# Where the node features are loaded and turned, and what the slot gathers signal on, in a two-layer graph kernel

## The reference, cut to what matters

```python
Hb = einsum('ni,bio->bno', h, V)
coef = w_comp[etype]
m = sum(coef[:, b] * Hb[b][src] for b in range(4)) * norm      # norm is edge_weight
agg = segment_sum(m, dst)
hn = relu(agg + h @ loop_w + bias)
y = hn @ ffn_w.T + ffn_b + h
x = layernorm(x + layernorm_with_gain(y))                      # first layer
x = layernorm(x + conv2(relu(conv1(x))))                       # attention over the edges
```

## Time and profile before

| what | us |
|---|---|
| median of 3 runs | 2035.97 (2034.86 to 2036.61) |
| the profiled execution | 2030.42 |
| its span in the profile | 2028.5 |
| TensorE matmul busy in the span | 1952.3 (96%) |
| VectorE busy | 1431.0 (71%) |
| ScalarE busy | 1297.1 (64%) |
| GpSimd busy | 671.6 (33%) |
| `message`, first row of the weight matrix built until the last feature sum | about 52 to 1057 |
| the two `conv` stages | 1067 to 1547 and 1548 to 2028 |

### The profile page before, as it was taken

One profiled execution on the slowest core, in us unless ns is written; L12 is line 12 of the kernel. 1 busy time (PEld: TensorE's weight loads), 2 busy tenths in 40 slices (PEclk: granted clock), 3 DMA queues, 4 the chain that ended last, 5 costly groups with the idle time before them and its releaser, 6 DMA issues. The chain is left out here.

```text
span 2028.5 us, 53132 instructions
## 1 busy us (share of the span) xinstructions
PE 1952.3 (96%) x19165; PEld 1633.2 (81%) x19165; DVE 1431.0 (71%) x4127; ACT 1297.1 (64%) x2289; POOL 671.6 (33%) x802
## 2 busy tenths in 40 slices
PE   1799999999999999999989999999999999999998
PEld 1789999999999999999975777777776777777777
DVE  3888878878887887888635666666663766677665
ACT  1566766767676676767645666666664666666665
POOL 3676577566657656665210000000000000000000
PEclk8899999999999999999999999999999999999999
DMA  3012111111211111121013222222211233222220
GB/s 80 9 38 76 42 40 52 65 39 39 77 40 40 53 64 39 39 78 37 34 67 128 96 69 90 95 95 84 73 63 71 94 104 103 84 87 101 102 102 8
DMA packets 43018, 137.00 MB, mean 68 GB/s; under 512 B 9190, under 2 KB 24359, under 8 KB 36484
## 3 DMA queue, kind: packets, MB, share of 16 engines
q1 hardware_dynamic: 38484, 128.24, 17.7%
q0 software_dynamic: 4400, 6.80, 1.4%
HBM read 91.83 MB, written 43.20 MB: 67 GB/s over the span
## 5 line engine op out<-in xcount | busy, mean ns | idle before, releaser
L854 PE MATMUL ps<-matrixT,x_rows 125*128 125x256 f32 (+1 forms) x2500 | 563.5, 377 | 0.1
L1703 DVE CUSTOM_DVE_ANT_0 scores_l<-ps,bias_rows_l 125x500 f32<-125x500 f32 (+1 forms) x700 | 396.6, 619 | 212.5 <-issue 212.5
L854 PEld LDWEIGHTS ps<-matrixT,x_rows 125*128 125x128 f32 x2500 | 461.3, 190 | 48.4 <-issue 0.2
L1608 ACT COPY weightsT_l<-ps 125x500 f32<-125x500 f32 x400 | 230.4, 577 | 293.4 <-PE ps L1514 292.8
L945 ACT COPY matrixT<-ps 125x500 f32<-125x500 f32 (+2 forms) x800 | 381.9, 652 | 44.3 <-PE ps L842 44.3
L1514 PEld LDWEIGHTS ps<-eye,scores_l 125*125 125x125 f32 x2500 | 287.8, 188 | 114.5 <-issue 106.7
L842 PE MATMUL ps<-high_weights,low_onehot 64*125 64x125 f32 x6300 | 368.2, 275 | 11.1 <-DVE high_weights L722 11.1
L842 PEld LDWEIGHTS ps<-high_weights,low_onehot 64*125 64x125 f32 x6300 | 357.9, 189 | 24.7 <-issue 15.8
L1514 PE MATMUL ps<-eye,scores_l 125*125 125x125 f32 x2500 | 324.9, 280 | 1.3 <-ACT weightsT_l L1608 1.3
L1600 ACT ACTIVATE scores_l<-scores_l,neg_max_l 125x1500 f32<-125x1500 f32 x200 | 318.0, 1594 | 7.5 <-DVE neg_max_l L1738 7.5
L1499 PE MATMUL ps<-kT_l,q_tile_l 64*125 64x500 f32 (+1 forms) x1400 | 317.0, 564 | 1.5 <-DVE chunk_max_l L1703 1.2
(11 more groups left out here) (152 smaller groups left out, 1725.7 us busy)
## 6 DMA issues: line engine op xcount, KB each, us to landing
bias_rows_l<-bias SPq DMA_DIRECT2D x50, 1562.5 KB, 6.7
bias<-bias SPq DMA_DIRECT2D x75, 500.0 KB
x_rows<-in_x SPq DMA_DIRECT2D x1, 1562.5 KB
bias<-bias SPq DMA_DIRECT2D x25, 62.5 KB
x<-x_rows SPq DMA_DIRECT2D x25, 62.5 KB
x_rows_l<-x SPq DMA_DIRECT2D x25, 62.5 KB
out<-rows_l SPq DMA_DIRECT2D x25, 62.5 KB
dst_int<-in_dst SPq DMA_DIRECT2D x1, 402.8 KB
```

The source lines that it names most:

```text
L854: last = nc.tensor.matmul(psG[:, BASES * SPLIT * side:BASES * (SPLIT * side + SIDE[side])], x[:, h, :], MT[side][:, 0:SIDE[side], BASES * ...
L1608: nc.scalar.copy(PT[i][:, 0:cw[c]], psT[i % 3][0:R, 0:cw[c]]).then_inc(z["pa_ok"], 1)
L1703: V.tensor_tensor_reduce(S[par][:, hd, lo:hi], psS[2 * ((par + j) % 2) + hd][0:R, 0:cw[j]], bias[par][0:R, lo:hi], 1.0, FLOOR, ALU.add, AL ...
```

## The change

The load of `x` leaves `prepare`. In `message` the sync engine issues it behind the 25 weight loads. (`prepare`'s other branch, for irregular graphs, which these inputs don't take, issues it ahead of its weights.) TensorE and ScalarE no longer turn `x` at the head of `message`; they do it in step 3, behind the first half of tile 0's pair products and their evacuation, and before the digits of tile 1 are turned. The seventh and eighth PSUM tile take the place of the first two. The four gathers of a tile's slots signal on two semaphores: destination and source on one, type and weight on the other. `slot_kinds` waits for the first, makes the digits, then waits for the second and makes `kinds`; `kinds_ok` is raised by the last row of `kinds`.

```diff
-def turn_inputs(nc, pe, m, turned_ps, turned_ok):
+def turn_inputs(nc, pe, m, turned_ps, turned_ok, at=0):
-    x, eye, ps = m["x"], m["eye"], m["ps"]
+    x, eye, ps = m["x"], m["eye"], m["ps"][at:at + 2]
...
-def turned_out(nc, act, m, turned_ps, turned_ok):
+def turned_out(nc, act, m, turned_ps, turned_ok, at=0):
-    xT, ps = m["xT"], m["ps"]
+    xT, ps = m["xT"], m["ps"][at:at + 2]
...   prepare, sync engine
-            sp.dma_start(m["x"][:, :, :], a["x"].rearrange("(t p) f -> p t f", p=R)).then_inc(m["x_in"], 16)
...   message
-        ell_in = [sem("ell_in0"), sem("ell_in1")]
+        near_in, kind_in = [sem("slot_ends_in0"), sem("slot_ends_in1")], [sem("slot_kinds_in0"), sem("slot_kinds_in1")]
...   message, gpsimd, find_slots
-                for to, name in ((e_dst, "dst"), (e_src, "src"), (e_type, "edge_type_8"), (e_weight, "edge_weight")):
+                for to, name, landed in ((e_dst, "dst", near_in), (e_src, "src", near_in), (e_type, "edge_type_8", kind_in),
+                                         (e_weight, "edge_weight", kind_in)):
...
-                                                 in_offset=bass.IndirectOffsetOnAxis(ap=slot_at[par][:, :], axis=0)).then_inc(ell_in[par], 16)
+                                                 in_offset=bass.IndirectOffsetOnAxis(ap=slot_at[par][:, :], axis=0)).then_inc(landed[par], 16)
...   message, sync engine
             load_weights(nc, sp, a, m)
+            sp.dma_start(m["x"][:, :, :], a["x"].rearrange("(t p) f -> p t f", p=R)).then_inc(m["x_in"], 16)
...   message, vector, search_row
-                    v.wait_ge(ell_in[par], half(s, par) * 64)
+                    v.wait_ge(near_in[par], half(s, par) * 32)
+                    v.wait_ge(kind_in[par], half(s, par) * 32)
...   message, vector, slot_kinds
-                v.wait_ge(ell_in[par], (half(s, par) + 1) * 64)
+                v.wait_ge(near_in[par], (half(s, par) + 1) * 32)
                 V.tensor_scalar(off[:, :], e_dst[par][:, :], node[par][:, :], OWN, ALU.is_equal, ALU.mult)
                 then(V.tensor_scalar(chunk[:, :], e_src[par][:, :], 1.0 / R, -0.496, ALU.mult, ALU.add))
                 then(V.tensor_scalar_add(chunk[:, :], chunk[:, :], MAGIC))
+                then(V.tensor_scalar_add(chunk[:, :], chunk[:, :], -MAGIC))
+                if not is_int(s) or s >= 2:
+                    v.wait_ge(digits_ps, s - 1)
+                V.tensor_copy(to[:, 1, :, :], twice(chunk[:, :]))
+                then(V.scalar_tensor_tensor(low[:, :], chunk[:, :], -float(R), e_src[par][:, :], ALU.mult, ALU.add))
+                V.tensor_tensor(to[:, 0, :, :], twice(low[:, :]), twice(off[:, :]), ALU.add)
+                v.wait_ge(kind_in[par], (half(s, par) + 1) * 32)
                 if not is_int(s) or s >= 1:
                     v.wait_ge(codes_ok, s)
                 for r in range(RELS):
-                    V.scalar_tensor_tensor(kinds[:, r, :], e_type[par][:, :], float(r), e_weight[par][:, :], ALU.is_equal, ALU.mult)
-                then(V.tensor_scalar_add(chunk[:, :], chunk[:, :], -MAGIC))
-                then(V.scalar_tensor_tensor(low[:, :], chunk[:, :], -float(R), e_src[par][:, :], ALU.mult, ALU.add))
-                if not is_int(s) or s >= 2:
-                    v.wait_ge(digits_ps, s - 1)
-                V.tensor_copy(to[:, 1, :, :], twice(chunk[:, :]))
-                V.tensor_tensor(to[:, 0, :, :], twice(low[:, :]), twice(off[:, :]), ALU.add).then_inc(kinds_ok, 1)
+                    last = V.scalar_tensor_tensor(kinds[:, r, :], e_type[par][:, :], float(r), e_weight[par][:, :], ALU.is_equal, ALU.mult)
+                last.then_inc(kinds_ok, 1)
...   message, tensor: the head loses the first two lines, step gains the last four
-            turn_inputs(nc, pe, m, turned_ps, turned_ok)
-            pe.wait_ge(turned_ok, len(TURNS))
...
                 if inside(w):
                     pair_products(w, 0)
+                if w == 0:
+                    pe.wait_ge(codesT_ok, 1)
+                    turn_inputs(nc, pe, m, turned_ps, turned_ok, 6)
+                    pe.wait_ge(turned_ok, len(TURNS))
...   message, scalar: likewise
-            turned_out(nc, act, m, turned_ps, turned_ok)
-            act.wait_ge(turned_ok, len(TURNS))
...
                 if inside(w):
                     evacuate(w, 0)
+                if is_int(w) and w == 0:
+                    turned_out(nc, act, m, turned_ps, turned_ok, 6)
```

## The result

The changed kernel takes 2043.59 us (median of 9 runs, 2040.69 to 2047.61) where the kernel before takes 2037.21 beside it (9 runs, 2034.86 to 2040.83): a ratio of 1.003, with a 95% interval of 1.0018 to 1.0041. The forecast was 2028.5, with 2025.0 to 2034.0 as its range for 8 in 10. The profiled run took 2040.69, with a span of 2038.8.

What follows compares the result with a forecast made beforehand. TensorE was taken to bound the loop, a serial chain up to the first one-hot the first 54 us. Gains 6.5 + 1.4 less 0.4 made 7.5, so 2035.97 - 7.5 = 2028.5 us, range 2025.0 to 2034.0 for 8 in 10.

Steps and rivals of the forecast that it cites:

- Part 1: At the branch: without the features queued ahead, tile 0's row gather is issued at 17.3 instead of 23.81; gain 6.5 us.
- my second rival: At the branch: DMA rings go round robin, so the late start has another cause and moving features gains nothing; 2035.0, chance 0.12.
- Part 2 at tile 0: Tile 0's slots: digits are done before the last gather lands, only the kinds stay behind; gain 1.4 us, bounds 0 and 1.55.
- Part 2 in the other 24 tiles: Loop: nothing gained, `kinds_ok` raised behind the same instructions, extra semaphore waits fall on VectorE with time to spare; 0.
- Part 3: Features issued behind the weights: they overlap tile 0's slot gathers, loss 0.4 us, and land in time for TensorE.
- Part 4: Turning the features in step 3: 6.0 us more on TensorE and ScalarE, covered by waits for VectorE's units; cost 0.
- the clock: TensorE's low granted clock, 0.60 at 72 to 74, may lie elsewhere; taken as 0, bounds -1.3 and +5 us.
- The rival of the clock: TensorE's low clock moves onto the feature sums, which nothing hides; price 5 of the 7.5, 2033.5, chance 0.12.
- The sum of the start: Tile 0's stall, slot and overlap terms together: 6.5 + 1.4 - 0.4 = 7.5 us gained.
- The base: Profiled execution of the kernel before, 2030.42 us; its 5.55 difference to the median of 2035.97 carried over unchanged.

Runs made afterwards that it cites:

- experiment 9: Kernel before with only the features' load and turning moved, but 12 of 25 feature tiles still loaded ahead of the branch; 2021.21 us beside 2027.53.
- 2: Kernel before with only the two semaphores and the new order in `slot_kinds`, features left in place; 2050.61 us, ratio 1.0052.
- 1: Kernel before with only the features' load and turning moved, one semaphore and old `slot_kinds`; 2034.87 us beside 2040.58.
- 12: Changed kernel with both semaphores, but all four waits at the head of `slot_kinds` and the old order in every tile; 2021.54 us beside 2027.53.
- 3: Changed kernel with the last digit instruction (low + off) put behind the kinds and raising `kinds_ok`; 2043.30 us, ratio 1.0017 to the kernel before.
- 6: Changed kernel plus one small VectorE memset between the last kinds and the edge-weight builds; 2030.77 us beside 2039.15 of the kernel before.
- 14: Changed kernel plus one small memset behind the kinds, repeated on another chip; 2022.62 us, ratio 0.9981 to the kernel before.
- 15: Changed kernel plus the same memset ahead of the kinds, before the wait for the second pair of gathers; 2029.05 us, ratio 1.0005 to the kernel before.
- 8: Kernel before plus one GpSimd addition ahead of each tile's coefficient products from the second tile on; 2047.32 us beside 2039.15.
- experiment 13: Changed kernel measured again without an edit; 2028.47 us beside 2027.12 of the kernel before, ratio 1.0007.
- experiment 4: Changed kernel with the new `slot_kinds` order in tile 0 only, the old order in tiles 1 to 24; 2033.72 us, ratio 0.9965 to the kernel before.
- 7: Changed kernel with the kinds put ahead of three digit instructions, which then raise `kinds_ok`; 2033.86 us beside 2039.15 of the kernel before.
- 11: Changed kernel plus two small memsets, on two tiles, behind the last kinds; 2020.76 us beside 2027.53 of the kernel before.

## Why the prediction was wrong, step by step

- **Part 1, the stall (6.5): the cause right, the size helped by luck.** The row gather moved from 23.81 to 18.08, 5.7; it was put at 17.3. The features' load was the cause: experiment 9 has half of it ahead of the branch, nearly through by then, and no added stall. What in the queue held the engines, their next instructions or something else, no run shows. Of the 5.7 only 4.5 are the stall (GpSimd's idle time there fell from 7.75 to 3.27), so that term was 2.0 too large. The other 1.25 is the flag, which came at 12.93 instead of 14.18 and which the text did not foresee. The Trainium skill's round robin ("DMA: Bandwidth & Descriptors", Queues, rings and completion order), taken as my second rival, would have left VectorE near 23; it began at 17.80. Another gain was not in the sum: VectorE read the gathered row 3.9 us after its issue (21.96 - 18.08) where the text had kept 6.8 and named the shorter one as 3.3 more.
- **Part 2 at tile 0 (1.4): right.** From the weights' landing to the first coefficient product it is now 32.67 - 31.39 = 1.28 us, where it was 2.72.
- **Part 2 in the other 24 tiles (0): this is the step that failed.** The text says that the digits now come first, "but `kinds_ok` is still raised behind the same instructions", and counts the instructions and waits: 0. They are the same instructions, but not the same ones next to GpSimd's first product and VectorE's builds. That turned the handover, at 12 us of loop on one level of chip (944.8 against 932.6; 945.7 and 946.3 against 934.9 and 934.2) and 7.3 on the other. Neither a rival nor the range had it; GpSimd does not appear in the text beyond tile 0, though the profile of before shows the collision in each tile: builds of 2.06 and 1.51 us beside GpSimd where the same lines take 1.19 and 0.98 alone. The steps behind it, each with its experiment: the order alone does it (2), the move and the waits don't (1, 12), the instruction that raises `kinds_ok` doesn't (3), a pause between kinds and builds undoes it (6, 14) and one ahead of the kinds doesn't (15), and a late GpSimd costs the loop by itself (8).
- **Part 3 (loss 0.4): right.** The weights landed 31.39 - 27.44 = 3.95 us after their issue against 3.61. The features were there when TensorE came at 54.73, 1.3 us before the 56 foretold.
- **Part 4 and the clock (0): the cost of 0 right, the clock at its good end.** From tile 0's first one-hot to tile 1's it is 31.75 us instead of 33.29, 1.5 less where the bound given was -1.3. The clock at 72 to 74 is 1.00 instead of 0.60, and 1.00 from 40 to 108 in both profiles of the changed kernel, though TensorE has gaps there too (it is busy for 54 of these 68 us). The rival of the clock did not come.
- **The sum of the start: 7.5 foretold, 9.6 at the first one-hot, 10.7 at the first y-product** in this profile (9.4 in experiment 13). Where the change is kept whole or nearly so and GpSimd gets its turn, the kernel is faster than the one before by 6.9, 8.4, 5.3, 6.8, 6.0 and 4.5 us (experiments 4, 6, 7, 11, 12 and 14), around the 7.5 of the forecast.
- **The base.** The trace that was read had a loop of 922.4, and the difference of 5.55 to the median was carried over unchanged. Part of it is that the loop differs by 10 us between the two levels.

What stays open: what decides the handover, and why on chips A and B the pair products take 9 us longer and the order costs 12 us instead of 7. The time by which GpSimd starts ahead of the build doesn't decide the handover: it is 0.10 to 0.12 us in some tiles and about 0.05 in the others, in losing and winning kernels alike (0.13 and 0.06 with the memset), and the outcome is the same in all tiles of a kernel. The start and the loop also don't add up to the time: -9.4 and +7.3 make -2.1 in experiment 13 where +1.4 was timed (-0.6 to +3.4), and -10.5 and +12.2 make +1.7 where +6.4 was (+3.7 to +8.3). The profiled run of the changed kernel was the fastest of its nine, and the start varies: the kinds of tile 0 began at 31.39 in one profile and at 33.52 in the other.

## What to carry to other kernels

When two engines that slow each other start together, the order of small instructions ahead of them is part of the schedule: in the trace of before, look for a line with two durations (here 2.06 beside GpSimd, 1.19 alone), ask which of the two engines can afford to be the one held, and give any reordering near that place a price on both sides. Apply a reordering that is meant for the first tile to the first tile only; experiment 4 did and was 6.9 us faster than the kernel before, without the loop's loss. And before a difference between two traces is explained, profile the old kernel a second time.

## What the runs showed of the hardware

- One instruction of 0.06 us between the kinds and the builds changed who was held for 2 us, in all 24 tiles: the first product is 3.12 us without it and 1.12 with it.
- The profiles of the kernels with the short first product fall in two levels for this loop: 922.4 to 923.2 us (first profile, C, D) and 932.4 to 934.9 (A, B), at the same granted clock of 1.00, with the same instructions; 9.1 us of it are the pair products (330.70 against 339.83). As each chip was used in one sitting, chip and sitting can't be told apart.
- At a branch VectorE, GpSimd and the sync engine stood still longer while a load issued ahead of it still ran: 9.27 us from the flag to VectorE's start with 1562.5 KB, 4.70 with 750 KB that were nearly through, 4.87 with none.
